# Other per-tile costs in the table that deals distance tiles to VectorE and ScalarE

## What is computed

```python
# layer 0: x = x + neg_l1(group_norm(x), W), W (128, 128, 3, 3)
P = patches(group_norm(x), 3x3, pad 1)            # (16, 128*9, 784)
neg_l1[b, f, l] = -sum_k abs(W[f, k] - P[b, k, l])
# layer 1: two 3x3 convolutions with quantised weights, batch norm, 4-bit activations, residual
# layer 2: additive (tanh) attention over the 784 tokens of an image, then a mixture of 8 experts
# layer 3: linear attention, then spectral filters
```

## Time and profile before

| what | us |
|---|---|
| median of 3 runs (12584.73 to 12590.29) | 12586.33 |
| the profiled execution | 12589.56 |
| its span, first to last instruction | 12587.8 |
| PE busy / DVE busy / ACT busy in the span | 11857.0 / 11395.9 / 10922.3 |
| granted TensorE clock, mean | 0.987 |

### The profile page before, as it was taken

The page is one execution under the profiler, slowest core; times in us unless marked ns, Lnnn a source line. Parts: engine busy times, 40 slices in busy tenths (PEclk is TensorE's granted clock), DMA queues, the critical chain, the costliest instruction groups (busy, mean ns, idle before and its releaser), DMA issues. The chain is left out here.

```text
span 12587.8 us, 298131 instructions
## 1 busy us (share of the span) xinstructions
PE 11857.0 (94%) x123040; PEld 5799.6 (46%) x123040; DVE 11395.9 (91%) x21555; ACT 10922.3 (87%) x7444; POOL 128.1 (1%) x103
## 2 busy tenths in 40 slices
PE   8999999999999999999767999999999999999999
PEld 3333333333333333333223555555555555555556
DVE  9999999999999999999899888889888898888881
ACT  8999999999999999999788888888888888888872
POOL 0000000000000000000000000000000000000000
PEclk9999999999999999999889999999999999999999
DMA  0000000000000000000110111111111111111113
GB/s 14 2 7 2 4 4 2 7 2 4 4 2 7 2 4 4 2 4 2 30 37 10 50 48 51 54 51 53 47 49 52 53 51 49 49 51 53 50 56 106
DMA packets 290040, 355.08 MB, mean 28 GB/s; under 512 B 28040, under 2 KB 242960, under 8 KB 288656
## 3 DMA queue, kind: packets, MB, share of 16 engines
q1 hardware_dynamic: 288656, 335.48, 9.1%
HBM read 314.14 MB, written 21.23 MB: 27 GB/s over the span
## 5 line engine op out<-in xcount | busy, mean ns | idle before, releaser
L276 ACT ACTIVATE c_ring<-c_xn,c_w_neg 128x1568 f32<-128x1568 f32 x3824 | 5791.7, 1604 | 282.2 <-PE c_acc L235 275.6
L235 PE MATMUL c_acc<-c_ring,c_onehot 128*32 128x392 f32 x68608 | 5764.6, 493 | 139.2 <-DVE c_ring L434 79.9
L1084 ACT ACTIVATE t_ring<-t_ring 128x3120 f32<-128x3120 f32 (+56 forms) x2160 | 4518.5, 2113 | 679.9 <-DVE t_ring L1406 667.2
L426 DVE TENSOR_SCALAR c_ring<-c_xn,c_w 128x1568 f32<-128x1568 f32 x4752 | 4573.5, 1036 | 95.5 <-PE c_acc L235 95.5
L1406 DVE TENSOR_SCALAR t_ring<-t_proj 128x784 f32<-128x784 f32 (+63 forms) x10240 | 3935.0, 457 | 573.4 <-PE t_psS L990 561.1
L235 PEld LDWEIGHTS c_acc<-c_ring,c_onehot 128*32 128x32 f32 x68608 | 2216.4, 110 | 3661.3 <-issue 3213.5
L990 PE MATMUL t_psS<-t_ring,t_vhot 128*32 128x392 f32 (+15 forms) x36864 | 2478.5, 402 | 154.7 <-ACT t_ring L1084 136.8
L947 PE MATMUL t_psC<-t_filter_work 128*128 128x392 f32 (+3 forms) x6144 | 1639.2, 401 | 8.1 <-ACT t_filter_work L1071 8.0
L990 PEld LDWEIGHTS t_psS<-t_ring,t_vhot 128*32 128x32 f32 x36864 | 1001.2, 111 | 1029.6 <-issue 367.9
L947 PEld LDWEIGHTS t_psC<-t_filter_work 128*128 128x128 f32 x6144 | 1133.2, 192 | 652.3 <-issue 32.9
L434 DVE SCALAR_TENSOR_TENSOR c_ring<-c_xn,c_w,c_ring 128x784 f32<-128x784 f32 x1280 | 1267.8, 1034 | 95.8 <-ACT c_ring L276 94.3
(11 more groups left out here) (227 smaller groups left out, 3405.2 us busy)
## 6 DMA issues: line engine op xcount, KB each, us to landing
t_filter_work<-in_toep_dram SPq DMA_DIRECT2D x256, 393.0 KB, 3.4
t_filter_work<-mix_scratch SPq DMA_DIRECT2D x512, 192.0 KB, 2.4
t_filter_work<-in_toep_dram SPq DMA_DIRECT2D x256, 197.0 KB, 2.6
t_filter_work<-mix_scratch SPq DMA_DIRECT2D x512, 64.0 KB, 1.8
mix_scratch<-t_filter_work SPq DMA_DIRECT2D x4, 2048.0 KB, 9.5
c_xin<-in_x_dram SPq DMA_DIRECT2D x8, 784.0 KB, 4.3
x_scratch<-c_x1o SPq DMA_DIRECT2D x8, 784.0 KB, 3.4
t_proj<-x_scratch SPq DMA_DIRECT2D x16, 392.0 KB, 3.5
```

The costliest lines, as they stand in the source:

```text
L235: mm = pe.matmul(acc[32 * g:32 * g + 32, ch, 0:HALF], onehot[:, 31 - r:63 - r], ring[:, s % RING, g, ch * HALF:(ch + 1) * HALF], start=(s ...
L276: ins = act.activation(tile4(ring[:, s % RING, g, :]), window(xn, tap), ACT.Relu, bias=w0_neg[:, tap, 4 * r + g:4 * r + g + 1])
L426: dve.tensor_scalar(tile4(ring[:, s % RING, g, :]), window(xn, tap), w0[:, tap, 4 * r + g:4 * r + g + 1], 0.0, ALU.subtract, ALU.max).then ...
L1084: act.activation(ring[:, st % RINGS, 0:n], ring[:, st % RINGS, 0:n], ACT.Tanh).then_inc(th.s, 1)
```

## The change

Three numbers of the table's cost model are others. The table is made anew from them, by the same rule.

```diff
-COST = dict(vec=0.95, act=1.55, merge=1.85)
+COST = dict(vec=0.962, act=1.514, merge=1.978)
```

## The result

| | us |
|---|---|
| changed kernel, median of 22 runs (12598.97 to 12610.18) | 12605.26 |
| kernel before, median of 22 runs (12580.02 to 12591.33) | 12585.34 |
| ratio, 95% interval | 1.0015 (1.0008 to 1.0022) |
| profiled execution / its span | 12604.54 / 12602.8 |

The change costs 19.9 us, or 0.16%. The interval lies wholly above 1, so the kernel is slower, but by less than the 0.2% that I had drawn as the border of "no change". I had forecast 12594, with 12558 to 12645 around it.

What follows compares the result with a forecast made beforehand. DVE was taken to bound the middle of each pair, PE the rest; ACT would become the bound. Tile and turn terms of -3.4 us and +12 us for ACT's stops made +8 us: 12594 us, range 12558 to 12645.

Steps and rivals of the forecast that it cites:

- The case: Whole kernel: no change, within 0.2% (25 us) of before; chance 0.60, and the forecast time is its own.
- its side: Whole kernel: slightly slower, by a sum of +8 us on the median of 12586.3.
- the sum: Distance loop: middle pairs -5.4, first pair -0.8, last pair +2.8, together -3.4; full ACT's losses +12; sum +8 us.
- The price of a tile: Distance loop, by starts: DVE 0.946, ACT 1.504, merge 1.89 us; the new costs overrate merges by 4.6%, ACT by 0.7%.
- The bound moves from DVE to ACT: Middle pair, steps 29 to 258: ACT becomes the bound, the length stays; PE begins step 258 0.4 us earlier.
- The turn of the pair: Between pairs: DVE makes 28 plain tiles behind the last merge, not 29; PE's last step comes last, 0.5 us gained.
- What a full ACT still loses: ACT's stops in each pair: between nothing and 12.8 us, taken as 1.5 us a pair, +12 us in all.
- the lower bound of nothing: First pair: ACT ran 172.68 us without a pause while DVE waited for it and PE starved, so no loss.
- The pair's readings: Distance between two readings of `acc`: stays near 764 us; the last pair's grows by 3.
- PE's first starving: Middle pair: PE first starves at step 41, some 1.5 us longer than before.
- The slower rival: Merges: ACT loses its lead, up to 12.8 us a pair, 12685 us (a third: 12617); chance of over +0.2%: 0.27.
- The faster one: Producers' stretch: DVE stays the bound, 12501 us; smaller form, cheaper ACT tile without stalls, 12559; chance of over -0.2%: 0.13.

Runs made afterwards that it cites:

- the V: Median change against the kernel before, by ACT tiles a pair: 478 tiles 0, 485 -39.0, 487 -21.1, 492 +19.9, 501 +91.4 us.
- Two experiments: Changed kernel with PE's eight box-sum matmuls left out: 12590.99 us; changed kernel with them spread behind steps 150, 162, 174, 186: 12590.33 us.
- The first three kernels with spread matmuls: Box matmuls spread in the changed kernel (12590.33 us), in the kernel before (12579.06), and in the kernel before with only ACT's cost at 1.514 (12537.74).
- the costs by starts: Kernel before with planner costs vec 0.946, act 1.504, merge 1.89, giving ACT 487 tiles a pair: 12564.43 us, ratio 0.9985.
- a deal with one at 99.7% and the other at 99.1%: Kernel before with only ACT's planner cost changed, to 1.514, giving ACT 485 tiles a pair: 12546.52 us, ratio 0.9971.

## Why the prediction was right, and where its sum was not

The case held, a time within 0.2% of before's, and so did its side: slower. It held with 5 us to spare, and one term of the sum, the stops of a full ACT, was a choice between 0 and 12.8 us a pair and not worked out stop by stop; that it came near enough is partly luck. By its own steps:

- *The price of a tile* held. 436 tiles at 1.504 us account for ACT's stretch to 0.4 us once its stops are taken off. The new costs agree with busy time over count, which has neighbours' overlap in it; that they favour ACT too much is borne out by the V, whose low point among the kernels run is at 485 tiles and not at 492.
- *The bound moves from DVE to ACT* held: 637.39 and 624.30 us, forecast 638 and 627. DVE's wait for ACT was forecast at some 10 us and was 15.4.
- *The turn of the pair* held in part. In the pair from 1552.29 to 2317.97 DVE's 28 tiles behind the last merge took 26.49 us (2291.48 to 2317.97) against 27.45, so some 0.95 us were won there and not 0.5.
- *What a full ACT still loses* is the term that was mis-sized, and the cause I gave for it was wrong. I took 1.5 us a pair, for slots and for DVE's lag at the merges. It is 2.6 us, and 2.41 of it is one stop that the eight box matmuls make: PE is 2.9 us late at one place, has 0.1 us a step to make it up (2.66 us of work in 2.77), and the ring lets ACT go only four steps ahead. Two experiments take this stop away in two ways, and each gives back 14 us of the 19.9 (23.4 and 19.6 us by the last reading). I had its trace before me, as the 2.5 us of the earlier trace rows, and put it to the merges' account. The 172.68 us of the first pair, from which I took the lower bound of nothing, end at 243.53, before that pair's box matmuls at 463.00; behind these the same trace has a stop of 2.54 us.
- *The pair's readings*: forecast near 764 us and 3 more for the last pair. The four plain pairs were 765.8, that is +1.8; the sum with 2.6 for stops and 0.95 for the turn gives -0.4 + 2.6 - 0.95 = +1.25. The last pair was +6.1 (2.8 + 2.6 = 5.4 by the sum with the right stop), the first +2.4 (-0.8 + 2.6 = 1.8). With 2.6 in place of 1.5 the whole sum is -3.4 + 21 = +17 us, and +15 with the turns' 0.95; measured were 19.9. Some 0.6 us a pair is thus not accounted for.
- *The two pairs that begin at a turn of the loop* rose together by 3.8 us more than two of the others. It lies between the reading and the first convolution: 25.85 and 25.57 us against 21.8 in the other pairs, where before it was 22.72 and 24.39. The first three kernels with spread matmuls show such an excess too, of 0.4 to 3.4 us, with no order in it. It was not tried by itself, so whether the change has a part in it stays open.
- *PE's first starving* came otherwise than forecast. Not step 41 was first but step 29, for 0.41 us, and step 30, for 0.80, because ACT makes all four tiles of step 29 and its merge comes late. Step 41's wait then was 0.39 us and not 1.5 us longer than before's 0.42. None of this mattered, since ACT, the bound, did not wait there.

The slower rival named the right kind of loss (a slot that comes back too late, which a full ACT can't regain) at the wrong place and price: it wanted 3.6 us a pair to decide, and 2.6 came. The faster one fell: ACT had no room for 14 tiles. It had room for seven.

## What to carry to other kernels

Price an instruction for a planner by the distance of starts in a long run without waits, not by recorded duration or busy time over count. Then judge the deal in the stretch in which both engines are full: the planner knows nothing of the stops, and here even the costs by starts gave ACT two tiles a pair more than the best deal that was run. When the bound is about to move to another engine, list that engine's stops before the change one by one and look at what the engine they wait for did just then: stops that were free until then become the cost. And where an engine takes its input from a short ring, spread its side work over many steps.

## What I had not expected of the hardware

At a turn of the loop PE loses up to 4 us, and not always the same: in the changed kernel the 256 matmul records behind it take 22.97 us instead of 21.27 (at 2320.92), and 2.34 us of idle time lie ahead. Only the two places where the loop turns show this, in all eleven profiles; what makes it was not tried. And two engines that are both nearly full (637.05 and 635.74 of 640 us) gave a slower kernel than a deal with one at 99.7% and the other at 99.1%: 12564 against 12547 us by the medians. A share of a window of fixed length does not tell how much work a pair holds, and only part of this lies in the distance loop: the last reading is 5.3 us later, a plain middle pair 0.8 us longer (759.3 against 758.6), and the rest of the program took 9.9 us longer in the one profiled execution of each.
